# A graph layer's in-degree counts on one Trainium2 core: four matmuls of 256 columns in place of sixteen of 64

## The reference

```python
row, col = (edge_index[0], edge_index[1])
h = jnp.concatenate([x[row], edge_attr], axis=1)
h = jax.nn.relu(_bn(h @ W1 + b1, g1, be1))
s = jax.ops.segment_sum(h, col, num_segments=n)
cnt = jax.ops.segment_sum(jnp.ones((h.shape[0], 1), h.dtype), col, num_segments=n)
agg = jnp.where(cnt > 0, s / jnp.maximum(cnt, 1.0), 0.0)
h2 = jnp.concatenate([x, agg], axis=1)
h2 = jax.nn.relu(_bn(h2 @ W2 + b2, g2, be2))
return jax.nn.relu(h2 @ Wl + bl)
```

## Time and profile before

| | |
|---|---|
| median of 3 runs | 865.92 us (861.46 to 869.04) |
| profiled execution | 868.43 us, its span 866.7 us |
| edge stage in the profiled execution | about 62 to 720 us |
| mean granted TensorE clock | 0.672 |
| busy in the span: PE / PEld / DVE / ACT / POOL | 412.7 / 325.3 / 384.1 / 205.6 / 448.0 us |
| chain that ended last | "another core or an unknown queue" 35%, PE 27%, issue 18%, DVE 7%, ACT 4% |

### The profile page before, as it was taken

How to read it: one execution, slowest core, us unless ns; L and a number is a source line. 1 busy time by engine, 2 the same in 40 slices (tenths; PEclk the granted TensorE clock), 3 DMA queues, 4 the chain that set the end, 5 groups by cost and what they waited for, 6 DMA issues and landing times.

```text
span 866.7 us, 11149 instructions
## 1 busy us (share of the span) xinstructions
PE 412.7 (48%) x2281; PEld 325.3 (38%) x2281; DVE 384.1 (44%) x792; ACT 205.6 (24%) x527; POOL 448.0 (52%) x540
## 2 busy tenths in 40 slices
PE   4732443325543234433244333445322627899985
PEld 4721322213332123322133222233211417899955
DVE  3533443334433234423344333444333546577785
ACT  1211111111111011111111111111111215466656
POOL 6346655566455575555665556646556355233330
PEclk9866666565556566655666655665566656899998
DMA  6323332223232223322233222333223324577702
GB/s 159 111 73 80 94 91 79 79 73 96 86 85 83 78 83 91 89 75 76 82 94 91 79 78 70 96 88 90 79 76 85 101 56 140 166 217 223 209 1 75
DMA packets 65246, 83.93 MB, mean 97 GB/s; under 512 B 19939, under 2 KB 43924, under 8 KB 65229
## 3 DMA queue, kind: packets, MB, share of 16 engines
q1 hardware_dynamic: 39885, 39.07, 16.1%
q0 software_dynamic: 13312, 27.29, 12.6%
q10 hardware_dynamic: 12032, 17.40, 5.6%
HBM read 63.62 MB, written 20.08 MB: 97 GB/s over the span
## 4 chain that ended last, share of the span: by engine, by line
another core or an unknown queue 35%; PE 27%; issue 18%; DVE 7%; ACT 4%; DVEq 3%; DMA 2%; ACTq 2%; POOL 0%; SPq 0%; POOLq 0%
PE psH L714 11%; PE psH L799 5%; PE psC L799 5%; ACT work L893 3%; DVEq L1094 2%; PE psT L708 2%; ACTq L910 1%; DVE res L1112 1%; DMA hotb<-hot_dram 1%; DMA res<-in_dst 1%; DVE cnt L1103 1%; DVE res L1235 1%; DVE psS L1119 1%; ACT res L322 1%
## 5 line engine op out<-in xcount | busy, mean ns | idle before, releaser
L605 POOL DMA_INDIRECT res<-ytab,srci x300 | 287.2, 957 | 97.9 <-issue 91.1
L714 PE MATMUL psH<-w1e,work 128*128 128x256 f32 x400 | 174.5, 580 | 327.3 <-ACT work L893 279.5
L714 PEld LDWEIGHTS psH<-w1e,work 128*128 128x128 f32 x400 | 101.8, 282 | 376.1 <-ACT work L893 300.5
L605 POOL DMA_INDIRECT work<-ytab,srci x104 | 100.0, 962 | 203.4 <-DVE res L1112 147.9
L1088 DVE TENSOR_TENSOR hotb<-iota,loc 128x256 bf16<-128x256 f32 x104 | 43.9, 422 | 252.5 <-remote 251.5
L893 ACT ACTIVATE work<-psT 128x256 f32<-128x256 f32 x104 | 39.9, 383 | 382.9 <-remote 294.8
L1126 DVE TENSOR_TENSOR psX<-work,psX 128x512 f32<-128x512 f32 x104 | 72.2, 694 | 43.3 <-ACT work L914 25.8
L914 ACT ACTIVATE work<-res 128x512 f32 (+1 forms) x78 | 49.1, 630 | 175.6 <-issue 97.6
L1204 DVE TENSOR_TENSOR work<-res,psX 128x512 f32<-128x512 f32 x103 | 70.7, 688 | 29.9 <-PE psC L799 15.1
L1112 DVE TENSOR_TENSOR res<-psH,res 128x512 f32 (+1 forms) x75 | 51.5, 687 | 30.6 <-PE psH L714 21.0
L628 POOL TENSOR_TENSOR agg<-agg,srci 128x64 f32 x104 | 32.2, 309 | 63.6 <-ACT srci L975 60.9
(11 more groups left out here) (164 smaller groups left out, 394.5 us busy)
## 6 DMA issues: line engine op xcount, KB each, us to landing
work<-in_edge_attr SPq DMA_DIRECT2D x103, 128.0 KB
hot_dram<-hotb ACTq DMA_DIRECT2D x26, 256.0 KB
spill<-work ACTq DMA_DIRECT2D x26, 256.0 KB
res<-spill SPq DMA_DIRECT2D x25, 256.0 KB, 3.1
res<-ytab,srci POOLq DMA_INDIRECT x300
hotb<-hot_dram SPq DMA_DIRECT2D x13, 256.0 KB, 2.7
work<-hot_dram SPq DMA_DIRECT2D x13, 256.0 KB, 3.4
h2x_dram<-agg ACTq DMA_DIRECT2D x25, 125.0 KB
```

Source lines behind the costliest of these rows:

```text
L605: pool.indirect_dma_start(rows[:, j * F:(j + 1) * F], None, ytab, bass.IndirectOffsetOnAxis(ap=srci[:, j, g:g + 1], axis=0)).then_inc(gath ...
L714: last = pe.matmul(psH[q % 2][:, b * 2 * F:(b + 1) * 2 * F], eat[:, q % 2, b * P:(b + 1) * P], w1e[:, :, :].rearrange("p a f -> p (a f)"), ...
```

## The change

`counts` loops over the four tile numbers j alone. Each matmul now takes tile j of all four groups as its moving operand, `hotb[:, :, j * WIN:(j + 1) * WIN]`: four pieces of 64 values, 512 bytes apart in each partition, 256 columns in all. Its output is `psC[0][:, 0:256]`, the same places as before. The matmuls of one cycle have 4 x 256 = 1,024 columns, as the 16 x 64 before. Operands, semaphores, and the order of everything else stay.

```diff
                 pe.wait_ge(hotb_ready, U * (i + 1))
                 if not (isinstance(i, int) and i == 0):
                     pe.wait_ge(cnt_added, U * i)
-                for q in range(U):
-                    for j in range(TILES):
-                        last = pe.matmul(psC[0][:, q * WIN:(q + 1) * WIN], onesb[:, :], hotb[:, q, j * WIN:(j + 1) * WIN],
-                                  start=(j == 0), stop=(j == TILES - 1))
+                for j in range(TILES):
+                    last = pe.matmul(psC[0][:, 0:U * WIN].rearrange("p (q w) -> p q w", q=U), onesb[:, :],
+                                     hotb[:, :, j * WIN:(j + 1) * WIN], start=(j == 0), stop=(j == TILES - 1))
                 for h in range(H2 if turned_out else 0):
                     last = pe.matmul(psC[0][:, U * WIN + h * PN:U * WIN + (h + 1) * PN], w2x[:, h * P:(h + 1) * P],
                               xt0[:, bass.ds(i * PN, PN)], start=True, stop=True)
                 last.then_inc(cnt_ps, 1)
```

## The result

The changed kernel takes 815.84 us (median of 6 runs, 812.59 to 818.62), the kernel before 865.48 us (6 runs, 861.46 to 869.04): a ratio of 0.9423, 95% interval 0.9388 to 0.9458. So it is faster by 5.8%, or 50 us, where 134 us were forecast.

A forecast was written before the change was run, and what follows sets the result against it. The prediction took late-delivered PE completions under POOL's gathers, in 23 cycles, to bound the kernel. Direct gain 0; removing 134.4 us of pauses from 868.4 gave 734.0, less 2.5 us to the median: 732 us, range 712 to 870 us.

The forecast's parts named there:

- 154.6 us of pauses: POOL's idle time before gathers behind DVE L1112: 147.9 us in 22 waits plus 6.74 us of the last.
- the direct cost: Counts on PE: columns stay 1,024, four matmuls take what sixteen took, 0.84 us to L761; direct gain 0.
- the two readings: What makes PE's completions late under gathers: number of instructions against an emptied limit, or PE's busy time emptied at 0.5 per us.
- nothing changes: Rival, chance 0.38: the trigger is something other than an emptied limit on PE's instruction number; time stays at 861 to 869 us.
- limit that only counts: Limit on PE's instructions since gathers began, never emptied meanwhile: the changed kernel's 51 is above 47, so still late.
- 20 of 23 gone: Edge stage: 20 of 23 cycles lose POOL's pause, 134.4 us of 154.6 us.
- r = 2: Rate per us at which PE's instruction limit is emptied under gathers; gives 29 for the changed kernel at the counts, on time.
- 51 - 11.23: Changed kernel at the counts: 51 PE instructions since gathers began, less 11.23 us times the emptying rate r.
- the limit of 37 to 47: PE instructions since a run of gathers began: 37 were on time, 47 late, so the limit lies between.
- without a pause: POOL's gathers would run on end if completions are on time: a cycle of 20.3 us rather than 26.7 us.
- a product alone never makes trouble: Ground for choosing the emptied limit: only instructions close together, as at the counts, are late; products beside gathers are on time.
- part of it: Rival, chance 0.12: a third of the cycles, or only one of the two completions, comes on time; 800 to 857 us.

The follow-up runs named there:

- e1: Counts made by 8 matmuls of 128 columns, 72 PE instructions per cycle; 695.8 us, ratio 1.0019 to the kernel before, on a chip where nothing is late.
- e3: Changed kernel counting only tile 0 by 4 matmuls of 64 columns; 694.82 us, ratio 0.9981 to the kernel before, on a chip where nothing is late.
- e6: Changed kernel with its four matmuls done four times over, 88 PE instructions per cycle, 4,096 columns; 858.63 us, ratio 1.0025 to the kernel before.
- e8: Kernel of e3 on a chip with late completions: 64 PE instructions per cycle, 256 columns; 821.3 us, ratio 0.9498 to the kernel before.
- e9: Kernel of e1 on a chip with late completions: 72 PE instructions per cycle, 1,024 columns; 850.98 us, ratio 0.9839 to the kernel before.
- e12: Kernel before with plain DMAs of 128 neighbouring rows from POOL's queue replacing indirect gathers from cycle 1 on; 562.4 us, ratio 0.8062.
- e17: Kernel of e12 once more, plain DMAs from POOL's queue, again on a chip where nothing is late; 563.52 us, ratio 0.8108 to the kernel before.
- e14: Changed kernel without the x @ W2 matmuls, 56 PE instructions per cycle; 697.32 us, ratio 0.9992 to the kernel before, where nothing is late.
- e18: Kernel of e14 once more on a third chip where nothing is late; 696.46 us, ratio 1.0004 to the kernel before.

## Why the prediction was right and wrong

**Right: what bounds the kernel.** The pauses were the late completions, and what was gained came out of them: 154.6 to 102.4 us of pauses, for a span 51.2 us shorter. On chips without them the kernel before takes 696 us, 170 us less; the prediction had 154.6 us of pauses in the edge stage. It left out the 13.1 us that end with the spill, which the trace of e1 does not have either.

**Right: the direct cost.** The four matmuls take what the sixteen took (24.1 and 24.0 us in the records; at 129.46 us L760 follows 0.85 us behind the first of them, as forecast), and where nothing is late e3 and e1 measure nothing from their form.

**Right: number, not busy time.** Of the two readings that ordered the rows equally well, e6, e8 and e9 decide for the number. The rival "nothing changes" (0.38) rested on the other reading, or on a limit that only counts; as a forecast it is refuted on the chips that show the trouble. That kernels close to the change measure nothing on three of the six chips of the experiments has a reason that was not in the forecast.

**Wrong: how much of it goes.** The step that failed is the term "20 of 23 gone" (134.4 us of 154.6 us), and under it the choice of r = 2 with a level that starts at nothing in every run of gathers. Measured, 52 of the 154.6 us went. Two things in that step were mis-sized.

First, the rate. In the stretch shown above four instructions came through in 4.1 us while gathers ran, and elsewhere in the changed kernel the counts' completion was seen by DVE at 178.48 us and that of the L708 behind it by ACT at 181.88 us: 3.4 us for four again. Near the limit the rate is about 1 per us, not 2. This trace has 33 stretches between two neighbouring starts of ACT's copy, DVE's L1111 or L1087 that both ended a wait of over 0.8 us, under running gathers: 216 instructions in 195.6 us, 1.1 per us, though single ones have from 0.7 to 7. PE makes 64 instructions per cycle, over 3 per us of POOL's 20.3 us. With 1.1 the prediction's own sum gives 51 - 11.23 x 1.1 = 39 for the changed kernel's first turn: at the limit, not clear of it.

```profile
181.88 0.38 ACT L892 ACTIVATE work<-psT 128x256 f32<-128x256 f32 x1 [10.29 <-remote]
```

```profile
178.48 0.42 DVE L1087 TENSOR_TENSOR hotb<-iota,loc 128x256 bf16<-128x256 f32 x1 [4.43 <-remote]
```

One of the slow ones runs from a copy of ACT to DVE's use of its product, eight instructions in 10.05 us:

```profile
346.91 0.38 ACT L892 ACTIVATE work<-psT 128x256 f32<-128x256 f32 x1 [3.15 <-remote]
```

```profile
356.96 0.69 DVE L1111 TENSOR_TENSOR res<-psH,res 128x512 f32 x1 [8.14 <-remote]
```

Second, and this did not need a new trace: the level at the end of a cycle was forgotten. Before, each cycle ended in a pause in which the store emptied, so counting from the start of a run was right. Take the pause away, and the next cycle starts from what the last one left. With the prediction's own r = 2 a cycle adds 64 - 2 x 20.3 = 23, and the limit of 37 to 47 is reached in the second; with r = 1 it adds 44 and is reached in the first or early in the second. A POOL that runs "without a pause" was never consistent with a store that is emptied fast only in a pause. The count over the whole trace agrees: the plain number since the last pause, or the number less 1.1 per us, has 3 of the 78 L708 on the wrong side of the best limit; with r = 2 it is 11 (in e8 10 and 16 of 81). The prediction's "a product alone never makes trouble" held only because the pause always came at the counts, ahead of it. The limit that only counts, which the prediction turned down, was the nearer one.

**Wrong with it: where the waits go.** The prediction looked for `hot_saved` or the spill as the next wait. It was the same late completion, at another instruction: 17 waits of DVE L1111 for a product, where the kernel before had none.

**Right for the wrong reason.** The case "part of it" (0.12, 800 to 857 us) holds the measured 815.84 us, and one of its grounds, that only some cycles lose the lateness, is what happened; that pauses then come at the products was not among them, so its holding the time is in part luck. With the level carried over it would have been the likely case, and it had 0.12. The overall range of 712 to 870 us holds the time too, but only because it reached for the unchanged case.

**The rule on ports.** The Trainium skill ("SBUF — State Buffer", Who interferes with whom) has TensorE waiting on nobody, from which no effect of the matmuls' number would follow. On the chips of e1, e12 and e17 the trace agrees: no remote wait at all. On the others the measurement decides against what would follow from it: ACT's copy waited 294.8 us for completions.

**Not settled.** Why some chips have it and others not, and whether it is the chip at all (only one was used twice, and had it both times); what of a gather holds the completions; what a "store" of some 40 instructions is: it is a picture that fits the number, most of the places and the effect of a pause, and no run shows the thing itself. Whether fewer than 64 instructions would gain more was asked twice (e14, e18), both times on a chip that could not answer. Whether weight loads count as much as matmuls was not tried; all edits changed both alike.

## What to carry to other kernels

When a wait is removed that also gave something time to empty, carry the level over into the next cycle before pricing the gain: ask in what state the new, pauseless loop starts its second turn. When completions of an engine are late although its work is done, count its instructions rather than its columns, and look at which queue falls silent just before they are let go; a deliberate gap there can be cheaper than the stall. And measure on more than one chip before a number is believed: the kernel before was 23 to 24% slower in four sets of runs than in three others.

## What the runs showed of the hardware that I had not expected

- The same kernel took 855 to 866 us on some chips and 695 to 697 us on others, with identical gathers (0.95 us each). Seven sets of runs fell on one side or the other, none between.
- Where it took 855 to 866 us, completions of PE are delivered late while POOL's indirect gathers run, once some 40 of its instructions have come since POOL's last pause; then about one per us gets through (1.1 on average over 33 stretches of the changed kernel, 0.7 in the slowest), and the rest together some 3 us after the last gather. A gap of 3.3 us in the gathers was enough to let them go, one of 2.3 us in most cycles was not.
- Adding 4 us of idle fills per cycle made the kernel before 6.1% faster there, and 13.7% slower on a chip without late completions.
- Four matmuls of 256 bf16 columns in pieces of 64, 512 bytes apart, stream like sixteen of 64 columns: 24.1 and 24.0 us in the records. From the first of them to the matmuls behind it are 0.85 us at a granted clock of 0.50 (129.46 to 130.31 us) and 0.45 us at 1.00 (104.19 to 104.64 us); before, 0.84 us (206.22 to 207.06 us) and 0.48 us (658.34 to 658.82 us) at the same two clocks.
